# Attention of a norm, FP4 and attention block: value products two steps at a time, with the order of events written out

## The reference, cut to what matters

```python
q = (x @ Wq.T).reshape(B, S, H, hd).transpose(0, 2, 1, 3)   # k, v alike; B=4, S=2048, H=16, hd=16
scores = jnp.einsum('bhqd,bhkd->bhqk', rope(q), rope(k)) * scale
scores = jnp.where(causal, scores, jnp.finfo(scores.dtype).min)
attn = jax.nn.softmax(scores, axis=-1)
out = jnp.einsum('bhqk,bhkd->bhqd', attn, v)
```

## Time and profile before

| what | us |
|---|---|
| median of 3 runs (2763.39 to 2765.77) | 2763.79 |
| the profiled execution, its own time | 2764.13 |
| its span, first to last instruction | 2762.3 |
| PE busy, matmuls | 2568.4 (93%) |
| DVE busy | 2335.1 (85%) |
| ACT busy | 1656.0 (60%) |
| two passes of attention, in the loop | 217.08 |

### The profile page before, as it was taken

The page is one execution under the profiler, slowest core; times in us unless marked ns, Lnnn a source line. Parts: engine busy times, 40 slices in busy tenths (PEclk is TensorE's granted clock), DMA queues, the critical chain, the costliest instruction groups (busy, mean ns, idle before and its releaser), DMA issues. The chain is left out here.

```text
span 2762.3 us, 55520 instructions
## 1 busy us (share of the span) xinstructions
PE 2568.4 (93%) x14690; PEld 1163.9 (42%) x14690; DVE 2335.1 (85%) x5197; ACT 1656.0 (60%) x3323; POOL 16.0 (1%) x7
## 2 busy tenths in 40 slices
PE   3699999999996899999999999999999999999979
PEld 2355556565553233333333333333333333333337
DVE  7889898888996888888898888888988988889803
ACT  2354544545542277777777767777777777667762
POOL 0000000000002000000000000000000000000000
PEclk8899999999997699999999999999999999999999
DMA  5111211112112301202111112011011111110017
GB/s 177 37 62 68 68 68 58 58 67 68 68 61 78 94 27 53 60 26 57 33 46 58 31 46 63 27 52 60 26 57 33 46 58 31 46 57 5 7 30 218
DMA packets 174761, 157.84 MB, mean 57 GB/s; under 512 B 53360, under 2 KB 153456, under 8 KB 174576
## 3 DMA queue, kind: packets, MB, share of 16 engines
q1 hardware_dynamic: 174576, 155.39, 18.3%
HBM read 95.81 MB, written 58.72 MB: 56 GB/s over the span
## 5 line engine op out<-in xcount | busy, mean ns | idle before, releaser
L1081 ACT ACTIVATE prob<-score 128x512 f32<-128x512 f32 (+3 forms) x2560 | 1189.6, 538 | 555.9 <-PE score L1017 313.0
L1125 DVE TENSOR_REDUCE top<-tile 128x1 f32<-128x512 f32 x1536 | 969.0, 684 | 116.7 <-PE tile L989 110.7
L989 PE MATMUL tile<-ks,qs 96*128 96x512 bf16 (+3 forms) x2560 | 852.3, 357 | 36.9 <-POOL ks L1105 20.8
L1012 PE MATMUL score<-qs,ks 99*128 99x512 bf16 (+3 forms) x2560 | 815.8, 350 | 19.8 <-ACT prob L1081 10.0
L1032 PE MATMUL acc<-prob,vs 128*32 128x512 f32 (+3 forms) x5120 | 600.2, 541 | 0.4 <-ACT prob L1081 0.4
L1130 DVE CUSTOM_DVE_ANT_0 tile<-tile,mask 128x128 f32<-128x128 f32 (+3 forms) x1024 | 473.0, 522 | 68.8 <-PE tile L989 63.4
L989 PEld LDWEIGHTS tile<-ks,qs 96*128 96x128 bf16 x2560 | 239.2, 98 | 536.5 <-DVE top L1125 207.8
L1012 PEld LDWEIGHTS score<-qs,ks 99*128 99x128 bf16 x2560 | 248.1, 98 | 369.7 <-ACT prob L1081 260.9
L360 PE MATMUL gu<-wguT,xT 128*128 128x512 f32 (+1 forms) x768 | 313.8, 562 | 20.7 <-DVE hid L668 20.7
L1017 PE MATMUL score<-identb,maskb 128*128 128x128 bf16 x1024 | 214.3, 221 | 3.2 <-issue 3.2
L360 PEld LDWEIGHTS gu<-wguT,xT 128*128 128x128 f32 x768 | 144.7, 192 | 167.6 <-issue 124.5
(11 more groups left out here) (101 smaller groups left out, 1746.8 us busy)
## 6 DMA issues: line engine op xcount, KB each, us to landing
qkp<-parts SPq DMA_DIRECT2D x192, 128.0 KB
qs<-qkp SPq DMA_DIRECT2D x384, 64.0 KB, 2.6
ks<-qkp SPq DMA_DIRECT2D x384, 64.0 KB, 2.5
vscr<-vt SPq DMA_DIRECT2D x16, 1024.0 KB, 4.5
vs<-vscr SPq DMA_DIRECT2D x16, 1024.0 KB, 6.2
x_all<-in_x SPq DMA_DIRECT2D x16, 512.0 KB, 8.9
oscr<-ot SPq DMA_DIRECT2D x64, 128.0 KB, 1.7
att<-oscr SPq DMA_DIRECT2D x64, 128.0 KB, 2.6
```

The lines of the kernel that those rows point to most:

```text
L989: mm = nc.tensor.matmul(bank[:, h * width:(h + 1) * width], qs[par][0:ROWS, h0 + h, q0:q0 + P], ks[par][0:ROWS, h0 + h, k0:k0 + width], st ...
L1012: mm = nc.tensor.matmul(bank[:, 0:width], ks[par][0:ROWS_M, h, kb * P:(kb + 1) * P], qs[par][0:ROWS_M, h, qb * GROUP + off:(qb + 1) * GROU ...
L1081: nc.scalar.activation(prob[:, k % PROB_SLOTS, 0:width], score[:, k % SCORE_SLOTS, 0:width], ACT.Exp, scale=HEAD ** -0.5).then_inc(probs_r ...
L1125: nc.vector.tensor_reduce(top[:, j, h0, c:c + 1], bank, AX.X, ALU.max).then_inc(tile_taken, 1)
```

## The change

The planner goes. The order of all events is a string `ORDER` of 348 letters: s takes the next entry of a list of scores and weighs, t the next tile (with the `top` that follows it, if one does), r a row, o an out. In the list of scores the weighs come in pairs: those of steps n - 2 and n - 1 stand behind the third score of each even step n, and the last pair behind all scores. With the string, 19 of the 20 pairs of a pass are adjacent in the plan, and the pair of steps 18 and 19 has two tiles and a row between its weighs. `prob` gets 16 slots, four steps of four, and the preset of `pv_done` goes from 2 to 4, on ACT, SP and GpSimd. The numbers of matmuls, exponentials, reductions and DMAs stay.

```diff
-TOP_APART, OUT_APART = 6, 3
-LAST_TILES = 4
-WEIGH_AT = 3
-MASK_WEIGHT = 1.5
+WEIGH_AT, WEIGH_STEPS = 3, 2
+ORDER = ("stsstttsssttstssstssstsstsstsstssttssrstststtsossttsstsstststtststsstststsststsststtstsstsssts"
+         "sttsssttsstssstssttstsosttstsssstststststtstsstssstssttssttststsssststsststtsstsstrtststsstssttt"
+         "sssssstssttssstrsstsststsststosstststsstststtststssttstsssstststtsstsstsssstssttsstrtsststssstst"
+         "sttstssttsstsssststststtsststsssststsststtststsssstssttssssto")
...
-    for n, (qb, kb, j) in enumerate(steps):
-        units = [[("scores", HG * n + h, n, qb, kb, j)] for h in range(HG)]
-        if n:
-            units.insert(WEIGH_AT, [("weigh", n - 1, *steps[n - 1])])
...
+    scores = []
+    for n, (qb, kb, j) in enumerate(steps):
+        for h in range(HG):
+            if h == WEIGH_AT and n and n % WEIGH_STEPS == 0:
+                scores += [("weigh", m, *steps[m]) for m in range(n - WEIGH_STEPS, n)]
+            scores.append(("scores", HG * n + h, n, qb, kb, j))
+    scores += [("weigh", m, *steps[m]) for m in range(n + 1 - WEIGH_STEPS, n + 1)]
...
+    for letter in ORDER:
+        if letter == "s":
+            plan.append(scores[scored])
+            scored += 1
+        elif letter == "o":
+            plan.append(("out", outs))
+            outs += 1
+        elif letter == "r":
             plan.append(rows.pop(0))
...
+        else:
+            plan.append(events[at])
+            at += 1
+            if at < len(events) and events[at][0] == "top":
+                rows.append(("row", *events[at][1:]))
+                plan.append(events[at])
+                at += 1
...
-    SCORE_SLOTS, TILE_SLOTS, PROB_SLOTS = 3, 4, 2 * HG
+    SCORE_SLOTS, TILE_SLOTS, PROB_STEPS = 3, 4, 2 * WEIGH_STEPS
+    PROB_SLOTS = PROB_STEPS * HG
...
-                    await_on(sp, sp_passed, pv_done, it * STEPS + STEPS + 2)
+                    await_on(sp, sp_passed, pv_done, it * STEPS + STEPS + PROB_STEPS)
...
-                act.wait_ge(pv_done, it * STEPS + e[1] + 1 + 2)
+                act.wait_ge(pv_done, it * STEPS + e[1] + 1 + PROB_STEPS)
...
-            for s, n in ((probs_ready, SCORE_SLOTS), (pv_done, 2), (acc_taken, 1), (tile_taken, TILE_SLOTS),
+            for s, n in ((probs_ready, SCORE_SLOTS), (pv_done, PROB_STEPS), (acc_taken, 1), (tile_taken, TILE_SLOTS),
```

More of the change, by code:

```diff
@@ L56 @@
 LEAD = 0.52
-TOP_APART, OUT_APART = 6, 3
-LAST_TILES = 4
-WEIGH_AT = 3
-MASK_WEIGHT = 1.5
+WEIGH_AT, WEIGH_STEPS = 3, 2
+ORDER = ("stsstttsssttstssstssstsstsstsstssttssrstststtsossttsstsstststtststsstststsstststsstststtsstsssts"
+         "sttsssttsstssstssttstsosttstsssstststststtstsstssstssttssttststsssststsststtsstsstrtststsstssttt"
+         "sssssstssttssstrsstsststsststosstststsstststtststssttstsssstststtsstsstsssstssttsstrtsststssstst"
+         "sttstssttsstssststststtsststsssststsststtststsssstssttssssto")
 class Chain:
@@ L762, in attention_plan @@
     steps = [(qb, kb, kb - 4 * qb if kb >= 4 * qb else None) for qb in range(QB) for kb in range(4 * qb + 4)]
[L764 to L780, removed]
-            plan.append(rows.pop(0))
@@ new lines, in attention_plan @@
+    scores += [("weigh", m, *steps[m]) for m in range(n + 1 - WEIGH_STEPS, n + 1)]
+    plan, rows, outs, scored, at = [], [], 0, 0, 0
+    for letter in ORDER:
[6 more added lines that the diff above has]
+        elif letter == "r":
+            plan.append(rows.pop(0))
+        else:
[5 more added lines that the diff above has]
+                at += 1
@@ L807, in attention_plan @@
+    assert scored == len(scores) and at == len(events) and outs == QB and not rows
     for qb in range(QB):
```

## The result

The changed kernel takes 2682.46 us (median of 4 runs, 2680.91 to 2682.97). The kernel before took 2764.44 in the same comparison. The ratio is 0.9701, 95% interval 0.969 to 0.9713: 3.0% faster. The forecast was 2680, the range 2662 to 2735.

What follows compares the result with a forecast made beforehand. PE was taken as the bound: its sum falls from 103.6 to 100.1 us, plus 2.75 of stalls is 102.85 a pass, 5.7 less. 15 x 5.7 = 85, less 1, from 2764.1 gives 2680 us, range 2662 to 2735.

Steps and rivals of the forecast that it cites:

- What bounds the kernel: Loop passes: PE bounds, its instructions sum to 103.6 us of a 108.54 us pass, the other 5.0 being stalls.
- The pair's 0.183: At each adjacent pair of weighs PE saves 0.183 us of switching; 19 pairs give 3.5 us a pass.
- The upper bound of 0.24: Most a pair could save, 0.091 + 0.145 us, if even the 0.03 between a weigh's halves goes.
- The stalls: PE's waits in a pass after the change: 1.0 + 0.4 + 0.85 + 0.5, about 2.75 us, down from 5.0.
- ACT's share: Stretches between pairs with too few tiles to cover ACT's five exponentials: about 1.0 us of stalls a pass.
- five stretches named: Stretches behind pairs of steps 26/27 (0.24), 16/17 (0.19), 0/1 (0.19), 18/19 (0.12) and 28/29 (0.09 us), short of tiles.
- The end of a pass: Weigh, copy of `acc`, out stays 1.21 us; with one tile less inside, 0.62 is open, plus 0.2 behind the out.
- the walk: Stretches with much masked work followed for DVE: each tile finds its bank free within 0.1; 0.4 us a pass allowed.
- The last pass: Without tiles, from about step 20, pairs take 5.2 us against 4.8, seven pairs lose 0.4 each: +1 us in all.
- The second: Rival: every weigh pays the switch again, so 3.5 us comes back and a pass is 106.3: 2732 us, chance 0.13.
- The first rival: The pair gains, the order doesn't; stalls stay at 5.0 us a pass: 2713 us, chance 0.24.
- The slower rival: ACT runs dry during pairs, 20 stretches losing 0.37 us each, a pass of 112.4: 2823 us, chance 0.06.

Runs made afterwards that it cites:

- the order alone: The change's written-out order with each pair's first weigh moved back to its old place, so no two weighs are adjacent: 2750.0 us, ratio 0.9945 to the kernel before.
- the pair alone: The planner of the kernel before, with the weighs of two steps put together and 16 slots of prob: 2775.38 us, ratio 1.0044 to the kernel before.

## Why the prediction was right, point by point

**What bounds the kernel**: right. PE set the time before, and its sum tells a pass to within the stalls.

**The pair's 0.183**: the mechanism was right, the size too low. Measured 0.231 (0.116 of the first weigh, 0.091 ahead of the second, 0.024 of the second). I had priced the change from weigh to weigh like the step between the halves, with its 0.03. But the 0.03 isn't paid at every half: it is paid once, behind the first half after a change from the full array. The upper bound of 0.24 was the nearer one. 19 x 0.048 = 0.9 us a pass are gained beyond the forecast. By the drain rule of the Trainium skill (TensorEngine Tiling (Array Packing), Key Properties) a pair saves all of it; the trace agrees, with 0.23.

**The stalls**: forecast 2.75, and over the same sum 2.79. The agreement is partly luck: the pairs' extra 0.9 hides in it, so the real stalls are 3.7. ACT's share was right, about 1.1 for 1.0. Of the five stretches named, those behind the pairs of steps 0, 18 and 26 show what was worked out (0.19 in step 3, 0.13 in step 21, 0.20 and 0.04 in step 30); the one behind step 28 shows 0.08, the one behind 16 only 0.04, the one with the copy of `acc`, behind step 11, 0.10 for 0.15, and 0.18 in step 2 was not foreseen. The end of a pass was right (0.63 + 0.25 for 0.62 + 0.2). DVE's was missed: 1.0 instead of 0.4, of which 0.54 in step 19, where the walk had found each bank free within 0.1. DVE ahead of the tile that PE could start only at 1507.16:

```profile
1500.22 1.94 DVE L1112 TENSOR_REDUCE top<-tile 128x1 f32<-128x512 f32 x3 [0.57 <-PE tile L976]
...
1504.81 0.22 DVE L1128 TENSOR_REDUCE topm<-top 128x16 f32<-128x64 f32 x1
...
1505.75 0.23 DVE L1133 TENSOR_TENSOR top_parts<-rest,top_parts 128x16 bf16<-128x16 f32 x1
1506.00 0.30 DVE L1117 CUSTOM_DVE_ANT_0 tile<-tile,mask 128x128 f32<-128x128 f32 x1
...
1506.96 0.14 DVE L1117 DVE_READ_ACCUMULATOR2_ANT top<- 128x1 f32 x1
```

From 1500.22 on DVE hardly pauses. It splits the maxima (the `top` event) for 1.2 us, from 1504.81 to 1506.00. Then it takes the tile that holds four heads of 128 columns in four pairs of instructions, 1.1 us until 1507.10, and this frees the bank. The prediction has a price for neither, only 0.5 for a masked tile of 384 columns.

**The last pass**: +1 was forecast, the trace gives -0.4. The full steps lose as worked out. PE, weigh to weigh, two steps:

```profile
2566.55 1.92 PE L1019 MATMUL acc<-prob,vs 128*32 128x512 f32 x16
2568.40 0.39 PE L999 MATMUL score<-qs,ks 99*128 99x512 bf16 x1
...
2571.76 1.07 PE L1019 MATMUL acc<-prob,vs 128*32 128x512 f32 x8
```

5.21 (2566.55 to 2571.76) stands against 5.2 forecast and 2 x 2.39 before. The pass's first half, with tiles, gained 2.3, and the second lost 1.9, less than 7 x 0.4.

**The signs named in advance.** Two passes took 205.78 for 205.7, and the 384-column tiles in step 20 start 0.17 ahead of their successors, as named. The second weigh starts 0.88 behind the first, not 0.91. DVE's wait for tiles fell to 9.0, not to "a few". ACT's idle time does lie in single gaps, 16 of them a pass, but most are 1.2 to 1.8 us long.

**The rivals.** The second was excluded by the row of the pair. The rule it leaned on, that loads overlap running matmuls only where row groups differ (the Trainium skill, TensorE: Matmul & The Clock Gate, The mechanism), doesn't fit: loads over the same rows start at 1503.44 and 1503.87 in the middle of running matmuls.

The first rival was wrong in its size and its sign: "the pair gains, the order doesn't" was priced at 2713 by keeping the old stalls, and the kernel that does just that takes 2775. The slower rival's mechanism is what happens there in five of twenty stretches, with 0.27 for one score and 0.35 to 0.41 over the stretch. I gave it the price of all twenty and no second cause. The burst in step 20 and the clock add 1.3 us a pass. So what the prediction lacked is that the old order's stalls are no constant. Its outcome was right since the change brings the order along: of the 82 us, the order alone gives 14, the pair alone takes 12, and 80 come only from both together. Why just this string keeps most of the old waits away is argued stretch by stretch, and only the places above were tested.

## What to carry to other kernels

Saving a fixed passage on the bounding engine pays only if its consumers' banks last through the longer block. Price the block against the banks (here 1.9 us against 1.4 us of scores and 2.4 us of tiles), and count what must lie between two blocks. Lay a burst of work for another engine around a single block, not ahead of a long one: here one weigh moved into the burst gave back 19 us. Putting the score first behind each pair cut four of the five local waits, and the kernel still lost 21 us elsewhere. Don't price an edit with the old stalls kept. A chain worked out at one place says what goes there and not what appears elsewhere: in three of four trials the repaired wait came back at another bank.

## What the runs showed of the hardware

FP32 matmuls over 32 of the array's columns, four at once, take 0.43 us for each recorded half of a full weigh. Behind the first half the next ones follow without a gap, with new weights or not (0.453, 0.429 and 0.430 from start to start). The way in and out costs 0.235 us once (0.091 + 0.026 + 0.118). The lower clock came behind a short row of PE waits, in passes in which PE is 97% busy: in the kernel with pairs alone PE waited 2.3 us in 3.6 us, and the granted clock was 0.53 in the next 3.3 us. The same place before, with 1.0 to 1.4 us of waits, stayed at full clock in every pass. Passes with the same waits are hit or not (0, 2, 6, 8 and 12 are, 4 and 10 are not), and the runs don't tell what decides it.
